# The first 512 keys reach the last 512 queries through a state: 160 made-up keys per head, whose pair products VectorE and GpSimd share

## The reference

```
q, k, v = norm(x) @ Wq.T, norm(x) @ Wk.T, norm(x) @ Wv.T
phi(u)  = [1, u / 2, u_i^2 / (4 sqrt 2), u_i u_j / 4 for i < j]
y_t     = sum_{s <= t} (phi(q_t) . phi(k_s)) v_s / (sum_{s <= t} phi(q_t) . phi(k_s) + 1e-12)
```

## Time and profile before

| | us |
|---|---|
| median of 3 runs | 3518.61 (3516.15 to 3518.98) |
| the profiled execution: its time | 3517.42 |
| its span, first to last instruction | 3515.6 |
| TensorE busy, by the profile | 3421.8 (97%) |
| ScalarE, VectorE, GpSimd busy | 2663.9, 2617.1, 1330.7 |

### The profile page before, as it was taken

One profiled execution on the slowest core, in us unless ns is written; L12 is line 12 of the kernel. 1 busy time (PEld: TensorE's weight loads), 2 busy tenths in 40 slices (PEclk: granted clock), 3 DMA queues, 4 the chain that ended last, 5 costly groups with the idle time before them and its releaser, 6 DMA issues.

```text
span 3515.6 us, 87647 instructions
## 1 busy us (share of the span) xinstructions
PE 3421.8 (97%) x32608; PEld 2412.3 (69%) x32608; DVE 2617.1 (74%) x8000; ACT 2663.9 (76%) x5724; POOL 1330.7 (38%) x1194
## 2 busy tenths in 40 slices
PE   7999999999699999999999999999999999999999
PEld 3433344333387878878788788787887888878877
DVE  3665556655678888888888888888888888888886
ACT  6789877898477777777777777777777777777775
POOL 2221112211434444444444444444444444444443
PEclk9999999999899999999999999999999999999999
DMA  7656766557322222222222222222222222222211
GB/s 157 140 135 126 145 147 137 102 105 133 109 66 65 61 73 66 67 70 61 72 67 64 70 64 68 70 61 72 65 67 71 62 72 66 62 73 66 69 46 42
DMA packets 289671, 293.21 MB, mean 83 GB/s; under 512 B 40928, under 2 KB 221280, under 8 KB 288736
## 3 DMA queue, kind: packets, MB, share of 16 engines
q1 hardware_dynamic: 289248, 287.62, 34.8%
HBM read 104.77 MB, written 58.73 MB: 47 GB/s over the span
## 4 chain that ended last, share of the span: by engine, by line
PE 72%; DVE 1%; POOL 0%; ACT 0%; issue 0%; DMA 0%; SPq 0%; DVEq 0%; POOLq 0%
PE f_ps L1357 18%; PE f_ps L1465 16%; PE f_ps L1477 9%; PE f_ps L1442 6%; PE f_ps L1421 4%; PE f_ps L1362 3%; PE f_ps L1384 3%; PE f_ps L1402 3%; PE f_ps L1431 2%; PE f_ps L1391 2%; PE f_ps L1470 2%; PE f_ps L1406 2%; PE f_ps L1449 1%; PE f_ps L1343 0%; DVE pr L1108 0%
## 5 line engine op out<-in xcount | busy, mean ns | idle before, releaser
L1028 POOL TENSOR_TENSOR turned<-qk,rot 128x256 f32<-128x256 f32 x512 | 403.7, 809 | 1250.3 <-ACT qk L1240 1236.2
L1357 PE MATMUL f_ps<-wqkv_s,hT 128*128 128x512 f32 x1536 | 706.8, 595 | 9.4 <-DMA hT<-xnT_dram 5.6
L1465 PEld LDWEIGHTS f_ps<-hnT,w_s 128*128 128x128 f32 x5120 | 591.7, 192 | 63.0 <-issue 59.8
L1465 PE MATMUL f_ps<-hnT,w_s 128*128 128x128 f32 x5120 | 592.5, 275 | 2.5 <-DVE hnT L1165 2.5
L1108 DVE CUSTOM_DVE_ANT_0 pr<-f_ps,masks_s 128x192 f32<-128x192 f32 x1024 | 326.1, 355 | 359.1 <-PE f_ps L1391 357.0
L545 ACT ACTIVATE weights<-t_ps,four_s 128x1024 f32<-128x1024 f32 x576 | 579.9, 1304 | 7.0 <-PE t_ps L653 6.6
L1273 ACT ACTIVATE pr<-pr,nmax,rnorm 128x192 f32<-128x192 f32 x1024 | 545.1, 535 | 44.3 <-DVE nmax L1115 44.3
L1357 PEld LDWEIGHTS f_ps<-wqkv_s,hT 128*128 128x128 f32 x1536 | 276.7, 190 | 273.8 <-issue 186.0
L1125 DVE TENSOR_SCALAR pr<-pr,rsum 128x192 f32<-128x192 f32 x1024 | 446.0, 497 | 9.0
L392 DVE SCALAR_TENSOR_TENSOR weights<-weights,causal_s 128x512 f32<-128x512 f32 x192 | 164.0, 868 | 279.7 <-ACT weights L545 279.2
L1477 PE MATMUL f_ps<-w_s,act_u 128*128 128x256 f32 x1536 | 352.7, 379 | 0.0
(11 more groups left out here) (119 smaller groups left out, 6288.7 us busy)
## 6 DMA issues: line engine op xcount, KB each, us to landing
vw<-vw SPq DMA_DIRECT2D x628, 128.0 KB, 2.4
qkT<-parts_dram SPq DMA_DIRECT2D x384, 128.0 KB, 6.1
kT<-kT SPq DMA_DIRECT2D x124, 256.0 KB, 2.7
parts_dram<-parts SPq DMA_DIRECT2D x64, 384.0 KB, 3.1
xnT_dram<-xnT SPq DMA_DIRECT2D x8, 1025.0 KB, 4.7
xs<-x_dram SPq DMA_DIRECT2D x8, 1024.0 KB, 8.0
xn_dram<-xn SPq DMA_DIRECT2D x8, 1024.0 KB, 5.4
attn_dram<-ao SPq DMA_DIRECT2D x8, 1024.0 KB, 10.3
```

Of the source, the lines that this page charges most:

```text
L1028: g.tensor_tensor(turned[:, heads, f], qk[:, heads, z], sines, ALU.mult).then_inc(done, 1)
L1357: last = mm(ps[:, b, :], rows, wqkv_s[:, l, c, i * INNER:(i + 1) * INNER], start=(c == 0), stop=(c == KC - 1))
L1465: last = mm(ps[:, UP[j // 2], o:o + P], w1_s[:, l, c, half * FULL + j * P:half * FULL + j * P + P], hnT[:, c, :], start=(c == 0), stop=(c ...
```

## The change

For queries of the second half (tokens 512 to 1023), the keys of the first half no longer go through scores. For each group of 4 heads, VectorE and GpSimd compute `psi`, 160 numbers for each of the 4 tiles of 128 past keys and each head: 120 products k_i k_j, 16 rows for squares, 16 for k itself, 8 for constants. GpSimd makes 66 of the products in 11 multiplications (`pairs`), VectorE 54 in 4 and the other rows in 6 more operations (`other_rows`). TensorE contracts psi with the values to a state (`state`, f32, 160 columns, accumulated over 4 tiles), VectorE copies it (`keep_state`), TensorE turns it round (`turn_state`), and VectorE copies it again. The queries meet 160 "made-up keys" (constant 0/1 sums `forms_s`), ScalarE squares these scores, and the state stands in the place of their values. A group thus has 5 near steps of two units, one unit without scores (the state), two units "past" and a single one of 512 numbers "rest", in this order.

Other parts of it: score matmuls use four 32-column strips, one after the other, instead of 128 columns; `psi` and `rest_w` share the memory of `parts`, so they wait for its stores; `project` computes k for 4 tiles in token rows too (2 more f32 matmuls of 256 columns a tile, a copy of 256 numbers on ScalarE); two small constants are loaded. Left out of the diff: allocations, the constants' values, the same counters renamed elsewhere, the waits of `pairs(b, 0)` and `other_rows(0)` for the k rows and for the stores of `parts`, and ScalarE's new loop, which squares the units in the order of UNITS.

```diff
+PAST = TILES // 2
+FORMS = P + VP
+SHARE = 4
+PAIRS_IJ = [(i, j) for i in range(TD) for j in range(i + 1, TD)]
+ROW_PAIRS, ROW_SQUARES, ROW_LINEAR, ROW_ONE = 0, len(PAIRS_IJ), len(PAIRS_IJ) + TD, len(PAIRS_IJ) + 2 * TD
...
-STEPS = [[(0, 0, 0)], [(0, 1, 0)], [(1, 0, P), (3, 0, 0)], [(1, 1, 0)], [(2, 0, 2 * P), (6, 1, 0)], [(2, 1, 0)], [(3, 1, 0)], [(4, 1, 0)],
-         [(5, 1, P), (7, 1, 0)]]
+STEPS = [[(0, 0, 0)], [(4, 1, 0)], [(1, 0, P), (3, 0, 0)], [(2, 0, 2 * P), (6, 1, 0)], [(5, 1, P), (7, 1, 0)]]
...
+        psi = space[:, 0:PAST * GH * FORMS].rearrange("p (th f) -> p th f", f=FORMS)
...
         NS = len(STEPS)
+        AS = NS + 1
...
+        UNITS = [(kind, i, pair) for kind, i, pair in
+                 [("near", i, pair) for i in range(NS) for pair in range(2)] + [("state", NS, 0)] +
+                 [("past", NS, pair) for pair in range(2)] + [("rest", NS, 0)]]
+        NU = len(UNITS)
+        SQUARES = NU - 1
...
+        DIAGONALS = {0: [(0, P)], 1: [(0, P)], 2: [(0, 2 * P)], 3: [(0, P), (2 * P, P)], 4: [(0, 2 * P)]}
+        LAST_STEP = [3, AS - 1]
...
+            def pairs(b, group):
+
...
+                k = krows[:, group].rearrange("p t h d -> p (t h) d")
+                for i in range(SHARE, TD - 1):
+                    o, width = PAIRS_IJ.index((i, i + 1)), TD - 1 - i
+                    last = g.tensor_tensor(psi[:, :, o:o + width], k[:, :, i:i + 1].to_broadcast([P, PAST * GH, width]),
+                                           k[:, :, i + 1:TD], ALU.mult)
+                last.then_inc(pairs_ready, 1)
+
+            def attention(b):
+                pairs(b, 0)
+                pairs(b, 1)
+                if b + 1 < B:
+                    root(b + 1)
+                pairs(b, 2)
+                normalise(b, 0)
+                pairs(b, 3)
+                normalise(b, 1)
+                normalise(b, 2)
 
             root(0)
...
+                def keep_state(g):
+                    group = b * GROUPS + g
+                    dve.wait_ge(state_ps, group + 1)
+                    v.tensor_copy(state_T, ps[:, unit_bank(g * NU + 2 * NS), 0:FORMS]).then_inc(state_kept, 1)
+                def turn_state(g):
+                    group, bank = b * GROUPS + g, unit_bank(g * NU + 2 * NS) + 1
+                    dve.wait_ge(turned_ps, group + 1)
+                    if group:
+                        dve.wait_ge(pv_done, group * AS)
+                    v.tensor_copy(state_main, ps[:, bank, 0:P])
+                    v.tensor_tensor(state_rest, ps[:, bank, P:2 * P], own_s[:, 0:P], ALU.mult).then_inc(state_ready, 1)
+                def other_rows(g):
+                    group = b * GROUPS + g
...
+                    k = krows[:, g].rearrange("p t h d -> p (t h) d")
+                    squares = psi[:, :, ROW_SQUARES:ROW_SQUARES + TD]
+                    for i in range(SHARE):
+                        o, width = PAIRS_IJ.index((i, i + 1)), TD - 1 - i
+                        v.tensor_tensor(psi[:, :, o:o + width], k[:, :, i:i + 1].to_broadcast([P, PAST * GH, width]),
+                                        k[:, :, i + 1:TD], ALU.mult)
+                    v.tensor_copy(psi[:, :, ROW_LINEAR:ROW_LINEAR + TD], k)
+                    v.reduce_sum(ksum[:, :], k, AX).then_inc(ksum_ready, 1)
+                    dve.wait_ge(ksum_ready, 4 * group + 1)
+                    v.tensor_scalar_add(ksum[:, :], ksum[:, :], 1.0).then_inc(ksum_ready, 1)
+                    dve.wait_ge(ksum_ready, 4 * group + 2)
+                    v.scalar_tensor_tensor(squares, k, 2.0, ksum[:, :].unsqueeze(2).to_broadcast([P, PAST * GH, TD]), ALU.mult, ALU.subtract)\
+                        .then_inc(ksum_ready, 1)
+                    v.tensor_scalar(psi[:, :, ROW_ONE:FORMS], ksum[:, :].unsqueeze(2).to_broadcast([P, PAST * GH, FORMS - ROW_ONE]),
+                                    -1.0 / (FORMS - ROW_ONE), 3.0 / (FORMS - ROW_ONE), ALU.mult, ALU.add).then_inc(ksum_ready, 1)
+                    dve.wait_ge(ksum_ready, 4 * group + 4)
+                    v.tensor_tensor(squares, squares, k, ALU.mult).then_inc(psi_rest, 1)
                 for g in range(GROUPS):
                     mask_diagonals(g, 0)
...
                     if following is not None and g == 0:
                         for t in range(4):
                             tile_stats(following, t)
-                    mask_diagonals(g, 2)
+                    mask_diagonals(g, 1)
+                    if g == 0:
+                        other_rows(0)
                     if following is not None:
                         if g == 0:
                             for t in range(4, TILES):
...
                         if g >= 2:
                             for t in range(2):
                                 layer_norm(following, (g - 2) * TILES // 2 + t)
-                    mask_diagonals(g, 4)
+                    mask_diagonals(g, 2)
                     if g >= 1:
                         invert_den(b, g - 1)
                     if following is not None and g >= 2:
                         for t in range(2, 4):
                             layer_norm(following, (g - 2) * TILES // 2 + t)
+                    mask_diagonals(g, 3)
+                    mask_diagonals(g, 4)
                     add_before(g, 0)
-                    mask_diagonals(g, 7)
-                    mask_diagonals(g, 8)
+                    keep_state(g)
                     if g >= 1:
                         spread_den(b, g - 1)
+                    turn_state(g)
+                    if g + 1 < GROUPS:
+                        other_rows(g + 1)
                 add_before(GROUPS - 1, 1)
...
+                if t < PAST:
+                    a.activation(krows[:, :, t, :, :], ps[:, 6 + t % 2, TH * TD:2 * TH * TD].rearrange("p (g h d) -> p g h d", h=GH, d=TD),
+                                 ACT.Copy).then_inc(krows_ready, 1)
...
+                for c in range(KC if t < PAST else 0):
+                    last = mm(ps[:, 6 + t % 2, TH * TD:2 * TH * TD], xnT[:, c, 1 + t * P:1 + (t + 1) * P], wqk_s[:, c, TH * TD:2 * TH * TD],
+                              start=(c == 0), stop=(c == KC - 1))
...
+                def state(n):
+                    g = n // NU
+                    group, bank = b * GROUPS + g, unit_bank(n)
+                    pe.wait_ge(pairs_ready, group + 1)
+                    pe.wait_ge(psi_rest, group + 1)
+                    for j in range(PAST):
+                        for h in range(GH):
+                            last = mm(ps[h * VP:(h + 1) * VP, bank, 0:FORMS], vals[:, j, g * GH + h, :], psi[:, j * GH + h, :],
+                                      start=(j == 0), stop=(j == PAST - 1))
+                    last.then_inc(state_ps, 1)
+                def turn_state(g):
+                    bank = unit_bank(g * NU + 2 * NS) + 1
+                    pe.wait_ge(state_kept, b * GROUPS + g + 1)
+                    for r in range(0, P, VP):
+                        mm(ps[r:r + VP, bank, 0:P], state_T[:, r:r + VP], id_s[:, :], start=True, stop=True)
+                    for r in range(0, P, VP):
+                        last = mm(ps[r:r + VP, bank, P:2 * P], state_T[:, P:P + VP], id_s[:, :], start=True, stop=True)
+                    last.then_inc(turned_ps, 1)
                 def scores(n):
-
-                    s, pair = n // 2, n % 2
-                    g, step = s // NS, STEPS[s % NS]
+                    g, bank = n // NU, unit_bank(n)
+                    kind, i, pair = UNITS[n % NU]
                     if n >= RING:
-                        pe.wait_ge(squared, 2 * first + n - RING + 1)
+                        consumed(n - RING)
                     else:
                         pe.wait_ge(rest_ready, b * BLOCKS + BLOCKS)
                         pe.wait_ge(before_ready, b + 1)
-                    if s % NS == 0:
+                    if n % NU == 0:
                         pe.wait_ge(qkT_in[g % 2], 16 * 2 * SLOTS * (2 * b + g // 2 + 1))
...
+                    if kind == "state":
+                        state(n)
+                        return
+                    if kind == "rest":
+                        for h in range(GH):
+                            last = mm(ps[h * VP:(h + 1) * VP, bank, :], forms_s[:, P:P + VP], qkT[g % 2][:, 0, h, 512:2 * 512], start=True, stop=True)
+                        last.then_inc(score_ps, 1)
+                        return
                     for k in range(2):
                         h = 2 * pair + k
-                        for j, half, o in step:
+                        if kind == "past":
+                            for r in range(0, P, VP):
+                                last = mm(ps[r:r + VP, bank + k, :], forms_s[:, r:r + VP], qkT[g % 2][:, 0, h, 512:2 * 512], start=True, stop=True)
+                            continue
+                        for j, half, o in STEPS[i]:
                             c = first_column(j, half)
```

(39 more changed lines are left out.)

152 lines of the change are left out of this document (101 added, 51 removed).

## The result

The changed kernel takes 3593.8 us (median of 4 runs, 3590.3 to 3598.9), the kernel before 3518.8 beside it: ratio 1.0216, 95% interval 1.0198 to 1.0233, 75 us slower. Its profiled execution spans 3588.4 us, 72.8 more than that of before.

The account below looks back on a forecast made before the run. ACT's squaring bounds attention, PE close behind. Attention +9.1 and `project` +3.4 make +12.5 us a sequence, +100 in eight, corrected to +101 on 3517.4: 3618 us. Forecast 3590 to 3650 (56%); 8 in 10: 3548 to 3675.

Parts of the forecast that it names:

- load wait: Groups 1 and 2: VectorE's reciprocal idles 4 to 5 us on the `den_flat` DMA, 16 times in all.
- rival A: VectorE is not stopped inside a group; the walk without load and port waits gives 69.8 us, so 3499; 5%.
- rival C: Only GpSimd's part costs; the small DMA does not stay behind the loads: attention 75.9 us, 3548; 6%.
- GpSimd's products: Eleven a group, 4.5 us on GpSimd; VectorE waits 1.8, 0.6 and 1.3 us in groups 0 to 2.
- the walk: One sequence's attention followed group by group, waits included: 84.6 us instead of 75.5, +9.1.
- `project` +3.4: In `project`, k in token rows for four tiles on PE adds 3.4 us a sequence.
- rival E: Four bf16 score strips do not run side by side: twice the price gives 3644, four times 3910; 6%.
- `normalise(1)` holds `other_rows(3)`, +2.3: Group 3: GpSimd's normalisation, starting when `spread_den` ends, holds VectorE's products; mask 0 done at 70.9 instead of 68.6.
- Corrections: Adjustments to +100: last sequence -2.5, scale tables in three sequences +6, last `spread_den` off the tail -2.6; sum +101.
- The DMA behind the loads: The small `den_flat` DMA stands behind a load's 12 DMAs; denominators arrive 13.9 us after the scores were done.
- The clock: Half-speed matmuls behind PE's waits could add up to 3 us a sequence; taken as nothing, kept for the range.
- B: Only the load wait is on the path, GpSimd's instructions fall into VectorE's idle time: attention 78.6 us, 3570; 15%.

Follow-up runs that it names:

- half_load: Changed kernel with half the bytes of each load of heads, leaving out queries and keys of the first 512 tokens: 3536.7 us.
- late_both: `late` plus both moves: group 0's layer-norm statistics off the masks' way, GpSimd's addition of two groups last: 3506.3 us, ratio 0.9961 to the kernel before.
- one_pair: Changed kernel with ten of GpSimd's eleven products of a group left out: 3584.8 us.
- own_queue: Changed kernel with the two small DMAs of the denominators issued on ScalarE's queue instead of SyncE's: 3601.8 us.
- spread_late: Changed kernel with only the two operations that spread the denominators moved behind `other_rows`: 3586.4 us.
- warm: Changed kernel with six unread matmuls of 256 f32 columns on PE where it waits for mask 3 in groups 1 to 3: 3621.8 us.
- late_add: `late` with GpSimd's addition of two groups behind the normalisation of group 2 instead of group 1, in all sequences but the last: 3522.3 us.
- late_order: `late` with group 0's layer-norm statistics moved from ahead of masks 1 and 2 to behind mask 3 and `turn_state`: 3525.8 us.
- late: Changed kernel with the denominators' reciprocal and spreading moved behind the copies of the turned state: 3537.3 us.

## Why the prediction was right, and where its steps were off

The mechanism held: the load wait is the largest part, with 16 stops where 16 were named, of 3.7 us where 4 to 5 were said, and masks 3 and 4, the state and PE behind it. `half_load` prices it at 57 us. The forecast's distance to a kernel without any stop (3618 less rival A's 3499) put load wait and GpSimd together at 119; `late_both`, in which some stops are left, lies 88 below the changed kernel. The total is 24 us below the forecast of 3618, near the lower edge of its 3590 to 3650. The forecast held 70 us for the load wait (3618 less rival C's 3548), 13 too many, and 30 for GpSimd's products (3.7 a sequence), of which `one_pair` finds 9. These two make 34, more than the 24: what the walk had too low or left out took some back, so that the total is closer than its terms, and that is luck. Point by point:

- **`project` +3.4:** +3.49, on the timeline. All of it is on the path: 28 us.
- **PE's prices:** as taken; 0.44 for a unit (0.88 for two), strips side by side (rival E is out).
- **The walk:** groups of 19.7, 21.5, 22.7 and 20.7, measured 19.9, 21.1, 22.0 and 19.8, so attention is 82.7 instead of 84.6. From a load to its reciprocal 13.1 us in the place shown against 13.9, and the chain from there to the last score 7.9 against 7.2.
- **GpSimd's products:** the mis-sized term. I let them cost VectorE 1.8, 0.6 and 1.3 us in groups 0 to 2; `one_pair` gives 9 us for ten of the eleven, 1.1 a sequence. VectorE's masks became 0.02 to 0.03 us longer than the earlier trace rows on average (717 for 689 ns, 1247 for 1225), not 0.3. Masks that all but keep their 0.69 are one of the two signs by which the prediction said that it would have failed, and this part of it did. Their own size was right: a group's eleven take 4.7 us on average, 4.5 forecast, 3.50 where VectorE leaves them alone and up to 5.57 where it does not. So it is mostly GpSimd that waits. (The prediction's lower end, with 0.12 us fixed, adds up to 3.1, not 3.6.)
- **`normalise(1)` holds `other_rows(3)`, +2.3:** the hold is 4.1 us (5.40 for 1.26); but group 3 took 0.9 us less than forecast, so some of it lay beside other work. The walk has no such hold of `other_rows(2)` by `normalise(0)`; it is 2.0 us (3.24 for 1.26), ahead of a group in which VectorE then waits for the load anyway.
- **Corrections:** last sequence and end together -5.1, measured -6.3 (from the last sequence's first score to the second part it is 0.6 us longer than before, against 6.9 in the others). The +6 for scale tables did not come: the trace has them in two sequences, not three (16 instructions of 0.42 us, b = 5 and 6), and these take 83.3 us on average against 82.5 of the other five; the kernel before shows the same step (76.4 for 75.6).
- **The DMA behind the loads:** that it lands late was right, the reason half wrong. I wrote that it stands behind them; `own_queue` shows that it waits as long in another queue, and `half_load` that the wait goes with the load's bytes. So it is the length of the load, whichever queue the small DMA is in. Rival C fails, and so would its remedy.
- **The clock:** left unpriced. It was at 0.85 over the phase instead of 1.00. It is inside the 57 us, where it cannot be much (groups 1 and 2 lose 8.2 us together in `half_load`, and VectorE had idled 7.4 in them; what is left, 0.8 us a sequence, holds all else that changed there), and inside the 7.1 us of `spread_late`; what it costs in group 3 stays open. That waits of 1.5 us leave the clock at 1.00 holds in the kernel before and in `half_load`, and does not in `warm`.
- **The rivals:** A's walk without stops gave 69.8 a phase and 3499. `late_both` has 70.8 and 3506: the relief of ACT and PE is there once VectorE's order lets it through. B (3570) was too cheap; what it lacks is probably the holds of the long GpSimd instructions (15 us for the addition, by `late_add`) and VectorE's order in group 0 (12, by `late_order`), but both were measured in `late`, not in the changed kernel.

What stays open: the slow clock's share in the remaining stops of groups 0 and 3, why group 3 is longer in `half_load` (21.0 for 19.8), and why a small DMA in a queue of its own is not served sooner.

## What to carry to other kernels

An instruction that waits for a DMA and was harmless late in an engine's order becomes the bound when the work ahead of it shrinks; when a change shortens an engine's round, every wait that the old round had hidden is to be timed against the new round, and moved before anything else is judged. A change that takes 28% of its work off the engine that bounds a phase (72.4 to 52.2 us) and makes the kernel slower is not a refuted idea: three moves of order turned +75 us into -14. And where two engines hold each other, look at the long instructions first: ten short ones a group cost 9 us here, one addition of 2.7 us a sequence cost 15.

## What the runs showed of the hardware

- A 16 KB DMA issued during a 12 x 128 KB load reached its reader 6.7 us later in the same queue and 7.6 us later in another (group 1 of the third sequence); with half the bytes in the load its reader waited 0.3 us in all, instead of 59.3.
- GpSimd's products cost nearly the same from 48 numbers to 176 (0.47 and 0.53 us), and less below: 0.32 for 32, 0.26 for 16 (means in the changed kernel, holds by VectorE included).
- PE stood for 1.8 to 2.2 us with no wait that the profile shows in three places of the changed kernel's first part, in or behind the state of group 2 of the first three sequences. In `late_order` there are seven such places of 0.6 to 2.6 us, in `half_load` none; the cause is not known.
